# A fused recurrence, attention and routing step: elementwise work moved off GpSimd, the gains g1 and b1 folded into the expert weights, router logits as extra matmul columns

## What is computed

```
xn  = layernorm(x)
pre = xn @ W + b ; i, f, o, z = split(pre)
per token t:  m' = max(f+m, i); i_s = exp(i-m'); f_s = exp(f+m-m')
              c = f_s*c + i_s*tanh(z); n = f_s*n + i_s; h = sigmoid(o)*c/(n+eps)
x   = x + h / rms(h) * scale                          # the cell
y   = layernorm(x)                                    # no gain
o   = causal attention(y @ w_qkv, 16 heads of 8) @ w_o
h   = layernorm(y + o) * g1 + b1
w   = top-2 of softmax(h @ wg), renormalised          # 8 experts
moe = sum_e w_e * (gelu(h @ w1[e] + bb1[e]) @ w2[e] + bb2[e])
out = x + layernorm(h + moe) * g2 + b2
```

## Time and profile before

| | |
|---|---|
| median of 3 runs | 1121.14 us (1109.04 to 1125.09) |
| profiled execution | 1105.74 us, span 1104.0 us |
| mean granted TensorE clock | 0.937 of full speed |
| busy share of the span | PE 86%, DVE 80%, ACT 64%, POOL 55% |
| DMA | 114.73 MB, mean 104 GB/s |

### The profile page before, as it was taken

The page is one execution under the profiler, slowest core; times in us unless marked ns, Lnnn a source line. Parts: engine busy times, 40 slices in busy tenths (PEclk is TensorE's granted clock), DMA queues, the critical chain, the costliest instruction groups (busy, mean ns, idle before and its releaser), DMA issues. The chain is left out here.

```text
span 1104.0 us, 26712 instructions
## 1 busy us (share of the span) xinstructions
PE 945.3 (86%) x7190; PEld 731.5 (66%) x7237; DVE 886.6 (80%) x2573; ACT 708.2 (64%) x1740; POOL 607.5 (55%) x797
## 2 busy tenths in 40 slices
PE   1467999999998998998999989950799999999574
PEld 1246677776775776776767766630799999999521
DVE  4568899999999999999999988576477777777368
ACT  2754888885885885885877646450466566566346
POOL 7211345445666766767858677586255565556400
PEclk9958999998999998999999999885799999999889
DMA  1024545353353353354343446142333332332096
GB/s 53 1 75 118 127 114 117 84 127 91 97 141 96 100 138 96 107 140 98 108 119 101 137 120 158 53 101 79 87 91 89 94 91 84 93 92 70 18 255 196
DMA packets 137975, 114.73 MB, mean 104 GB/s; under 512 B 19314, under 2 KB 126456, under 8 KB 137860
## 3 DMA queue, kind: packets, MB, share of 16 engines
q1 hardware_dynamic: 120772, 92.24, 32.4%
q0 software_dynamic: 8640, 16.93, 4.8%
q10 hardware_dynamic: 8448, 4.20, 1.3%
HBM read 60.60 MB, written 52.58 MB: 103 GB/s over the span
## 5 line engine op out<-in xcount | busy, mean ns | idle before, releaser
L595 POOL TENSOR_SCALAR_AFFINE_SELECT b_PT<-b_PT 128x256 f32<-128x256 f32 (+1 forms) x384 | 194.9, 525 | 179.2 <-ACT b_PT L776 175.4
L1125 DVE TENSOR_REDUCE b_m_neg<-b_ps_m 128x2 f32<-128x512 f32 (+1 forms) x384 | 257.5, 678 | 38.9 <-PE b_ps_m L1542 21.1
L776 ACT ACTIVATE b_PT<-b_ps_s 128x512 f32<-128x512 f32 x384 | 221.8, 601 | 42.6 <-PE b_ps_s L1518 21.7
L1874 POOL DMA_INDIRECT results<-e_Y,e_X x142 | 148.5, 1045 | 125.3 <-DVE e_Y L1941 102.4
L630 POOL DMA_INDIRECT slots<-c_pay,b_pos x128 | 129.9, 1015 | 36.9 <-issue 26.2
L1989 PE MATMUL e_ps_d<-e_h,e_w 128*128 128x256 f32 x568 | 135.0, 381 | 0.0
L1521 PE MATMUL b_ps_s<-c_QK 128*128 128x512 f32 x256 | 114.7, 450 | 8.9 <-ACT b_PT L776 8.9
L1542 PE MATMUL b_ps_m<-c_QK 128*128 128x256 f32 x512 | 119.9, 323 | 0.0
L1901 ACT ACTIVATE e_h<-e_ps,e_w 128x256 f32<-128x256 f32 x284 | 111.4, 480 | 0.8 <-PE e_ps L1980 0.8
L1989 PEld LDWEIGHTS e_ps_d<-e_h,e_w 128*128 128x128 f32 x568 | 103.0, 191 | 11.2
L1535 PE MATMUL b_ps_m<-c_QK 128*128 128x128 f32 x512 | 100.1, 320 | 7.9 <-DMA c_QK<-qk_scr 7.9
(11 more groups left out here) (242 smaller groups left out, 2418.7 us busy)
## 6 DMA issues: line engine op xcount, KB each, us to landing
c_QK<-qk_scr SPq DMA_DIRECT2D x128, 192.0 KB
qk_scr<-b_qk_hi SPq DMA_DIRECT2D x64, 256.0 KB, 2.5
e_X<-slots SPq DMA_DIRECT2D x71, 130.0 KB, 2.3
qk_scr<-b_qk_lo SPq DMA_DIRECT2D x32, 256.0 KB, 2.7
f_G<-results SPq DMA_DIRECT2D x32, 256.0 KB, 3.7
a_X<-in_L_attn_x_dram SPq DMA_DIRECT2D x16, 256.0 KB, 6.2
x<-a_X SPq DMA_DIRECT2D x16, 256.0 KB, 2.8
b_X<-x SPq DMA_DIRECT2D x32, 128.0 KB, 5.4
```

Source lines behind the costliest of these rows:

```text
L595: nc.gpsimd.affine_select(out=tri, in_=tri, compare_op=ALU.is_ge, fill=0.0, base=0, pattern=[[0, tri.shape[1]], [1, P]], channel_multiplie ...
L776: nc.scalar.activation(PT[:, g % 2, q % 3], ps_s[:, q % 2], ACT.Exp, scale=HD ** -0.5).then_inc(s_e, 1)
L1125: nc.vector.tensor_reduce(out, scores, AX.X, ALU.max, negate=True).then_inc(s_red, 1)
L1874: nc.gpsimd.indirect_dma_start(dram["results"][:, :], bass.IndirectOffsetOnAxis(X[:, j.of(NB_X), u, D:D + 1].bitcast(u32), 0), Y[:, n, u, ...
```

## The change

- The affine part of the norm after attention is left out of the fused step. ACT writes (R - mean) * rstd straight into both copies of the payload (`hidden_norm`, two activations of 128x256 output with a bias and a scale column). g1 is multiplied into the rows of w1 and into the residual term of the experts (L1934 before); w1^T b1 is added to the first bias and b1 to the second.
- `rows_norm` goes from DVE to ACT too. DVE computes only the small tiles -mean * rstd (`rows_shift`, `hidden_shift`).
- Logits: the router's weights times g1, centred, are 8 extra columns of the value projection and, multiplied by w_o, of the output projection, so that the residual R is 136 wide and its last 8 columns are the logits but for the factor rstd and a constant. POOL applies these two (`logits`, two instructions of 128x16). The transposition, its copy, the logits' matmul and their copy are gone.
- The roots of the three norms (cell, in, out) lie side by side: one Ln and one Exp a step, at the step's end (`roots`).
- Cell: `cell_path` (DVE) computes u = M(t-1) + sp in place, `cell_input` u - i; ACT makes both exponents by Relu of that with either sign (`cell_part_i`, `cell_part_f`), and the exponentials follow one step later. POOL has no part in it.
- Cell's rms norm: `cell_back` is four plain transpositions; ACT squares them with its accumulator (four activations, each waiting for the one before); DVE multiplies by the rms and by scale; POOL adds x (`cell_rows`, 128x512), and SP's store waits for that.
- Routing: the lag is 7 or 8 steps, and for the first four groups `route_weights`, `ranks` and `route_slots` come one or two steps after `route_first`. There are 45 steps instead of 46.
- Each engine has six orders instead of two: for the filling steps (s below 4), the full ones and the last ones (s from 32), each even and odd.

The core of the diff; `...` marks what is left out:

```diff
-ROUTE_LAG = 8
-SEND_LAG = 9
+ROUTE_LAG = 7
+ROUTE_STEP = [c + ROUTE_LAG + (c % 2 if c < 20 else 0) for c in LAST]
+SLOT_STEP = [min(s + 2, ROUTE_STEP[q + 1] - 1) if LAST[q] < 18 else s for q, s in enumerate(ROUTE_STEP)]
+DX = D + E
...
 # GpSimd
-            def cell_forget(g):
-                nc.gpsimd.tensor_tensor(f_s, cell.M[:, :, 0:T], sp, ALU.add).then_inc(c_fsum, 1)
-                need(pool, c_fsum, g + 1)
-                nc.gpsimd.tensor_tensor(f_s, cell.M[:, :, 1:T + 1], f_s, ALU.subtract).then_inc(c_fa, 1)
+            def cell_rows(g):
+                need(pool, c_y, g + 1)
+                nc.gpsimd.tensor_tensor(cell.X[:, g.of(NC)], cell.Y[:, :, :], cell.X[:, g.of(NC)], ALU.add).then_inc(c_x1, 1)
-            def rows(d):
-                nc.gpsimd.tensor_tensor(H1[:, :, :], H0[:, :, :], g_b[:, :, :].to_broadcast([P, 2, D]), ALU.mult).then_inc(s_h1, 1)
-                nc.gpsimd.tensor_tensor(pay[:, r, :, :, 0:D], H1[:, :, :].unsqueeze(2).to_broadcast([P, 2, TOPK, D]), ...
+            def logits(q):
+                nc.gpsimd.tensor_tensor(LS[:, :, :], R[:, :, D:DX], rstd1[:, :].unsqueeze(2).to_broadcast([P, 2, E]), ALU.mult).then_inc(s_ls, 1)
+                nc.gpsimd.tensor_tensor(L[:, q.base], LS[:, :, :], bw[:, :, :].to_broadcast([P, 2, E]), ALU.add).then_inc(s_L, 1)
 # ScalarE
+            def hidden_norm(q):
+                for t in range(2):
+                    last = nc.scalar.activation(pay[:, r, t, :, 0:D], R[:, t, 0:D].unsqueeze(1).to_broadcast([P, TOPK, D]), ACT.Identity,
+                                                bias=shift1[:, t:t + 1], scale=rstd1[:, t:t + 1])
+            def rows_norm(a):
+                for t in range(2):
+                    last = nc.scalar.activation(XN[:, a.of(NB), t, 0:D], X[:, a.of(NX), t, :], ACT.Identity,
+                                                bias=shift[:, t:t + 1], scale=rstd[:, t:t + 1])
+            def roots(s, n, p, g):
+                for a, b in root_runs(s.base):
+                    nc.scalar.activation(logs[:, a:b], means[:, a:b, 1], ACT.Ln, bias=eps_ln[:, :]).then_inc(s_log, 1)
+                for a, b in root_runs(s.base):
+                    nc.scalar.activation(roots_of[:, a:b], logs[:, a:b], ACT.Exp, scale=-0.5).then_inc(s_root, 1)
+            def cell_part_i(g):
+                nc.scalar.activation(cell.i_s[:, :], cell.sp[:, :], ACT.Relu, scale=-1.0).then_inc(c_ri, 1)
+            def cell_part_f(g):
+                nc.scalar.activation(cell.f_s[:, :], cell.sp[:, :], ACT.Relu).then_inc(c_rf, 1)
             def cell_rms(g):
+                for t in range(4):
+                    need(act, c_ss, 4 * g + t)
+                    nc.scalar.activation(cell.sq[:, :], ps_r[:, t * P:(t + 1) * P], ACT.Square, accum_out=cell.ss[:, t:t + 1]).then_inc(c_ss, 1)
 # VectorE
+            def cell_path(g):
+                nc.vector.tensor_tensor(sp, cell.M[:, :, 0:T], sp, ALU.add).then_inc(c_u, 1)
             def cell_input(g):
+                nc.vector.tensor_tensor(cell.sp[:, :], cell.sp[:, :], cell.i[:, :], ALU.subtract).then_inc(c_ia, 1)
+            def rows_shift(a):
+                nc.vector.scalar_tensor_tensor(out=shift[:, :], in0=mv[:, :, 0], scalar=-1.0, in1=rstd[:, :],
+                                               op0=ALU.mult, op1=ALU.mult).then_inc(s_sh, 1)
 # TensorE
-            def cell_sums(g):
-                    last = nc.tensor.matmul(ps_r[:, t:t + 1], cell.C[:, t * P:(t + 1) * P], cell.one_col[:, :], start=True, stop=True)
             def cell_back(g):
-                    last = nc.tensor.matmul(ps_r[:, t * P:(t + 1) * P], cell.H[:, t * P:(t + 1) * P], cell.diag[:, :], start=True, stop=True)
+                    last = nc.tensor.transpose(ps_r[:, t * P:(t + 1) * P], cell.H[:, t * P:(t + 1) * P], ident[:, :])
 # experts, VectorE
-                        nc.vector.tensor_scalar(XW[:, u, :], X[:, m, u, 0:D], X[:, m, u, D + 1:D + 2], None, ALU.mult).then_inc(s_xw, 1)
+                        nc.vector.scalar_tensor_tensor(out=XW[:, u, :], in0=X[:, m, u, 0:D], scalar=X[:, m, u, D + 1:D + 2], in1=kept["g1_b"][:, :],
+                                                       op0=ALU.mult, op1=ALU.mult).then_inc(s_xw, 1)
```

1232 lines of the change are left out of this document (777 added, 455 removed).

## The result

The kernel after takes 1143.8 us (median of 4 runs, 1139.0 to 1145.92) beside 1123.12 us of the kernel before (4 runs, 1109.04 to 1130.94): 1.0221 times as long, 95% interval 1.0118 to 1.0324. A second sitting gave 1.0128 (1.0069 to 1.0186). It is 1 to 2% slower, where 5% faster was forecast, outside the range and on the wrong side.

The account below looks back on a forecast made before the run. DVE was taken to set a pair's pace, PE close behind; PE bounds the experts. Full steps -34.7, last steps -8, tail -8, filling 0, experts +1 give -49.7: 1056 us, 1071 scaled, 1063 forecast; range 1035 to 1108.

Parts of the forecast that it names:

- The engines' work: Busy time in an ordinary pair of full steps: DVE 36.2 to 33 us, ACT 31.0 to 34.9, PE 38.0 to 35.1.
- weights and ranks come two steps later: Routing steps such as 11: ACT's stall of 3.05 us goes; step 11 within 2 us of step 13.
- The squares: Cell's rms norm on ACT: four squares with accumulator at 0.38 us each, +1.5 us a pair, bounds 0.8 and 2.2.
- the keys' way through memory: Odd full steps: reads behind the cell's store start some 2 us later; 1.5 us a pair show, bounds 0 and 2.5.
- 12 for the rest: Full steps: of 28.3 us beyond ordinary pairs, 12 stay, for some 24 small DVE instructions a group in five groups.
- The tail: Last exponential to experts: POOL products, transposition and a step of sends go; -8 us, bounds -3 and -13.
- the expert biases that PE now makes there stand beside the sends: Tail: PE's new bias work runs beside the sends; no separate cost given.
- The last steps: Nine steps after the full ones: PE loses 0.7 us and POOL 2 us a step; -8 us, bounds 0 and -16.
- Experts: Experts' stage: 142 instructions reading two tiles, each about 0.07 longer, beside PE's work; +1 us, bounds 0 and +10.
- Rival 3: Full-step pair stays 38.2 us because the keys' reads take all of the gain; 1092 us, chance 0.08.
- Rival 4: ACT's in-order queue keeps its waits, deciding from 3.3 us of remaining waits a pair; slower, 1132 us, chance 0.05.
- Rival 1: POOL still blocks DVE's two-input SBUF instructions, three meetings of 0.7 us; pair 37.6 us, 1068 us, chance 0.20.

Follow-up runs that it names:

- g2: Kernel after with the store behind the reads, expert biases and weights' scaling later, and PE's maximum(b, 0) and maximum(b, 1) later in even full steps: 0.9772 of before.
- k4: Kernel after with only two of the four query and key reads from the fourth batch on, half of the heads using stale data: 0.9751 of before.
- m2: Kernel after with store behind reads, biases, weights' scaling and maximum(b, 0) later, run again on another chip without the routing split: 0.9718 of before.
- c1: Kernel before, unchanged, profiled a second time: 0.9996 of before, full steps 468.2 us.
- m1: Kernel after with store behind reads, biases, weights' scaling and maximum(b, 0) later, plus two more groups' weights, ranks and slots in later steps: 0.9712 of before.
- h1: Kernel after with the cell's sum made earlier in odd full steps on VectorE and GpSimd, store still ahead of the reads: 1.0097 of before.

## Why the prediction was wrong

**The engines' work was forecast rightly.** In steps 6 and 7 with nothing late (g2) VectorE is busy 32.9 us (forecast 33), ScalarE 34.4 (34.9), PE 35.5 (35.1). The pair takes 37.0 us there and 35.9 with half of the reads; the forecast's pair without its term for the keys was 35.1. Step 11 fell to the length of its neighbours, as "weights and ranks come two steps later" had it. The squares were under-sized: 1.5 us, measured 1.1 and 0.8, since each has a second instruction that reads the accumulator (group by line, g2, steps 6 and 7):

```profile
L824 ACT ACTIVATE a_sq<-a_ps_r 128x128 f32<-128x128 f32 x4 | 1.1, 286 | 0.1
...
L824 ACT ACTIVATION_READ_ACCUMULATOR a_sq<-a_ps_r 128x1 f32 x4 | 0.8, 206 | 0.0
```

**The step that failed is "the keys' way through memory".** It was named as the cover that could be gone, in the right steps and with the right list of waits to show it, but its size was "1.5 us a pair show, bounds 0 and 2.5". Measured over the full steps: 38.8 us, 3.4 a pair. Three errors made it. (1) The wrong one of two times was worked out. The forecast has the reads start "some 2 us later"; against the step they start 0.4 us later (0.7 us ahead of its first exponential instead of 1.1). In the kernel after they are bound by the last score of the batch whose buffer they fill, and by the store for 0.4 us more. In the kernel before the forecast's `b_qk_lo` did bind them, in the step shown and in eight of eleven even steps, but the row of zeros, which the score releases, went out only 1 us earlier (304.12 and 305.09), and I had not looked at what that row waits for. (2) The time at which PE asks was left where it was in the step. The new order has `maximum(b, 0)` behind score 4, the old one behind score 7, so PE asks 4.5 us into the even step instead of 8.3, and the 9.2 us of the earlier trace rows between reads and use became 5.5 against a transit of 7.7. This is the larger part. Both orders were there to be read. (3) A stall was priced as its own length. It also lowers the granted clock: 0.87 in step 6 of after against 1.00 without the stall, and 12 us of PE's busy time in all. The Trainium skill says as much in TensorE: Matmul & The Clock Gate, section HAM oscillation — how this bites in real kernels, that waits for DMAs between bursts of matmuls bring the clock down again and again. By that rule these rows agree, and the term would have been larger had I asked what a wait does to the work behind it.

Against a forecast of -34.7 us, the full steps gave +10.2, a miss of 44.9. The forecast held 17.3 us for the keys (1.5 a pair). Their arrival cost 38.8 (k4), which is 21.5 more. The other 23.4 are in k4 too: it takes 439.0 where the forecast without the keys is 415.6. Of these, 6.6 are its first full step, where the first batches still make all reads (27.5 us against 20.9 in step 6). Another 9.2 are the pair, 35.9 instead of 35.1, eleven and a half times: PE is busy 0.4 more and idles 0.4. The last 7.6 are the extra time beyond such pairs, 19.6 where 12 were left: most odd steps from 13 on take 15.6 to 16.5 us instead of 15.0, and step 25 takes 20.3. So the work of each engine was right, but taking the busiest engine's time for the pair, and 12 for the rest, was too little.

**The tail**, forecast -8, gave +0.8. "The expert biases that PE now makes there stand beside the sends" was wrong: they stood ahead of the last batch's values in PE's queue. Moved, the tail was 41.0 us, -6.3 against before. **The last steps**, forecast -8, gave +5.3. The forecast took PE's and GpSimd's work off them and did not ask for the keys there. With half of the reads they take 149.2 us, 3.0 less than before, so by these two profiles the keys are the larger part of it, in the steps 32 to 35. In m2, where PE waits 10.6 us for the keys in steps 27 to 35, these take 156.7 us, against 149.5 of before in c1. Why 27 to 31 take 93 to 99 us in the profiles of the new kernels and 88 to 91 in those of before stays open; it is not the two groups' routing (m1). **Experts**, forecast +1: 260.4 against 259.4 where no slots were slow, right; the 18 us seen at first are the slow slots.

**The rivals.** Rival 3 had the right mechanism, "the keys' reads take all of the gain", with a chance of 0.08 and a bound, 38.2 a pair, that the runs passed (41.5). Rival 4, ScalarE's queue, needed more than 3.3 us of remaining waits: with 34.4 us of work it idles 2.6 in g2's pair of 37.0, so it does not decide. It is near, though: with the keys out of the way, the longest of PE's waits in g2's full steps are for ScalarE's exponentials, 10.3 us in 21. Rival 1, blocking: in that pair the new product of VectorE and its neighbour take 681 ns each, as an undisturbed one did, so no blocking shows there (VectorE's groups, g2, steps 6 and 7):

```profile
L1184 DVE TENSOR_TENSOR a_sp<-a_M,a_sp 128x512 f32<-128x512 f32 x1 | 0.7, 681 | 0.0
L1191 DVE TENSOR_TENSOR a_sp<-a_sp,a_i 128x512 f32<-128x512 f32 x1 | 0.7, 681 | 0.0
```

## What to carry to other kernels

When an order changes, price each transfer by the distance in time between its issue and the instruction that asks for it, in the new order: first find what allows the issue (here, after the change, the last reader of the buffer and not the producer of the data), then where the asking instruction now stands. Busy times that fall or stay within their room say nothing of a loop through memory whose length stays. Price a wait of PE with the lower clock behind it. And when a DMA is moved in a queue, look at what it lets through: here the store's landing also decides when the next loads start, and whether they travel beside reads that somebody waits for.

## What was not expected of the hardware

Four reads of 192 KB landed 7.7 us after the first one's issue where 384 KB of loads were issued about 2 us behind it, and 7.0 us where a store of 256 KB stood in the loads' place (medians). A store issued 3.4 us ahead of the reads had ended its transfer before they began and did not lengthen them (h1, 7.7 as in the kernel after). The same program spent 259.4 or 282.9 us in the experts, with ScalarE idle 0.8 or 31.9 us ahead of the same activations; the six profiles on two chips all had 0.8, the eight on a third 6.6 to 31.9. A profile from one execution can miss, or hold, 20 us that are no property of the kernel.
